# Graph layer on one core: seven of thirteen products of x with Wn1 moved behind all products for A and B

## The reference

```
msg_in   = concat(x[src], x[dst])
h        = relu(relu(msg_in @ Wm1 + bm1) @ Wm2 + bm2)
messages = h @ Wm3 + bm3
agg      = segment_sum(messages, dst) / max(count, 1)
upd      = relu(concat(x, agg) @ Wn1 + bn1) @ Wn2 + bn2
out      = layernorm(x + (x + upd))
```

## Time and profile before

| what | value |
|---|---|
| median of 3 runs | 1199.37 us (1196.93, 1199.37, 1199.49) |
| profiled execution, its time | 1197.71 us |
| its span, first to last instruction | 1195.5 us |
| PE busy | 1159.5 us (97%) |
| DVE busy | 975.5 us (82%) |
| POOL busy | 795.2 us (67%) |
| ACT busy | 743.9 us (62%) |
| mean granted clock of PE | 0.993 |

### The profile page before, as it was taken

The page is one execution under the profiler, slowest core; times in us unless marked ns, Lnnn a source line. Parts: engine busy times, 40 slices in busy tenths (PEclk is TensorE's granted clock), DMA queues, the critical chain, the costliest instruction groups (busy, mean ns, idle before and its releaser), DMA issues.

```text
span 1195.5 us, 33711 instructions
## 1 busy us (share of the span) xinstructions
PE 1159.5 (97%) x9565; PEld 1139.2 (95%) x9566; DVE 975.5 (82%) x2097; ACT 743.9 (62%) x1378; POOL 795.2 (67%) x827
## 2 busy tenths in 40 slices
PE   6888999999999999999999999999999999999996
PEld 6778999999999999999999999999999999999886
DVE  5876877788788888888888888888888888887897
ACT  3555666666666666666666666666666666664674
POOL 2057777777777777777777777777777777773021
PEclk8999999999999999999999999999999999999999
DMA  8876656666565666656666666666555666653022
GB/s 286 306 288 187 179 176 177 176 183 182 180 176 174 180 182 180 181 171 180 182 181 179 174 178 181 178 184 179 175 177 179 181 181 177 174 180 97 19 80 92
DMA packets 136608, 211.47 MB, mean 177 GB/s; under 512 B 25125, under 2 KB 103673, under 8 KB 135034
## 3 DMA queue, kind: packets, MB, share of 16 engines
q1 hardware_dynamic: 99034, 108.50, 29.7%
q0 software_dynamic: 37536, 102.55, 29.0%
HBM read 188.15 MB, written 22.80 MB: 176 GB/s over the span
## 4 chain that ended last, share of the span: by engine, by line
PE 88%; DVE 4%; issue 2%; SPq 2%; POOL 2%; DMA 1%; ACT 0%; DVEq 0%
PE bank L1451 45%; PE bank L1427 14%; PE bank L1338 8%; PE sums L1355 4%; PE sums L1361 4%; PE sums L1359 4%; PE sums L1363 4%; PE bank L1493 2%; POOL a_edge L631 2%; PE bank L1248 1%; DMA a_table<-work 1%; PE sums L1503 1%; PE bank L1233 1%; PE sums L1233 1%; DVE work L1144 1%
## 5 line engine op out<-in xcount | busy, mean ns | idle before, releaser
L631 POOL DMA_INDIRECT a_edge<-a_table,src_idx x782 | 759.7, 971 | 246.7 <-issue 209.9
L1451 PE MATMUL bank<-w,h 128*128 128x256 f32 x4692 | 615.7, 280 | 0.0
L1451 PEld LDWEIGHTS bank<-w,h 128*128 128x128 f32 x4692 | 580.5, 188 | 0.0
L740 ACT ACTIVATE h<-bank 128x512 fp32r<-128x512 f32 x391 | 234.3, 599 | 311.4 <-PE bank L1338 305.2
L1103 DVE SCALAR_TENSOR_TENSOR h<-bank,h 128x512 fp32r<-128x512 f32 x391 | 269.1, 688 | 108.8 <-ACT h L740 72.6
L1115 DVE SCALAR_TENSOR_TENSOR h_lo<-bank,h_hi 128x512 fp32r<-128x512 f32 x391 | 266.6, 682 | 0.0
L729 ACT COPY bank<-b_bc 128x512 f32<-128x512 f32 x391 | 231.6, 592 | 51.4 <-DVE h_lo L1115 46.5
L1427 PE MATMUL bank<-ident,a_edge 128*128 128x128 f32 x1564 | 235.2, 273 | 7.0 <-DVE onehot_t L1020 5.6
L748 ACT ACTIVATE h_hi<-bank 128x512 fp32r<-128x512 f32 x391 | 233.2, 596 | 2.8 <-PE bank L1451 2.8
L1020 DVE TENSOR_SCALAR onehot_t<-rel,node_half 128x256 fp32r<-128x256 int16 x391 | 143.9, 368 | 67.6 <-DMA b_win<-b_table 52.2
L1338 PE MATMUL bank<-onehot_t,b_win 128*128 128x256 f32 x782 | 189.5, 323 | 0.0
(11 more groups left out here) (188 smaller groups left out, 682.4 us busy)
## 6 DMA issues: line engine op xcount, KB each, us to landing
b_win<-b_table SPq DMA_DIRECT2D x391, 128.0 KB
rel<-rel_dram SPq DMA_DIRECT2D x196, 128.0 KB
a_edge<-a_table,src_idx POOLq DMA_INDIRECT x782
a_table<-work SPq DMA_DIRECT2D x12, 512.0 KB, 4.3
b_table<-work SPq DMA_DIRECT2D x5, 1024.0 KB, 5.4
b_table<-h SPq DMA_DIRECT2D x4, 1024.0 KB, 5.5
f_x<-in_x SPq DMA_DIRECT2D x12, 256.0 KB, 5.8
b_table<-a_edge SPq DMA_DIRECT2D x3, 1024.0 KB, 6.1
```

What stands on the lines that cost most here:

```text
L631: pool.indirect_dma_start(a_edge[:, b % R * TB + t, :], None, a_table, bass.IndirectOffsetOnAxis(ap=src_idx[:, b * TB + t:b * TB + t + 1], ...
L740: act.activation(h1[:, k % U, 0, :], bank[k % 2][:, :], ACT.Relu).then_inc(s_h1h, 1)
L1451: ins = pe.matmul(to, h1[:, j, a, h * EB + t * P:h * EB + (t + 1) * P], w2[:, b, h, :], start=False, stop=(a == 1 and h == KH - 1), skip_g ...
```

## The change

Groups 0 to 5 of x @ Wn1 are still made inside the setup's iterations, one each in 5, 7, 8 and 9 and two in iteration 6. Groups 6 to 12 stand behind all products for A and B: groups 6, 7 and 8 ahead of the product W3 x Wn1, groups 9 to 12 behind it. They use banks 6 and 7 and banks 2 and 3 in turn, so that a product waits for the copies of the one before the last. The wait for the last copy of A (s_ac) stands ahead of group 7 now. SP waits for the product of group 6 before it loads windows of B, since the ring of windows holds that group's split x.

```diff
-        TWICE = (XA, XA + 3)
+        EARLY = NG - XB
+        X_AT = {XA: [0], XA + 1: [1, 2], XA + 2: [3], XA + 3: [4], XA + 4: [5]}
         def x_groups(g):
-            done = max(g - XA, 0) + sum(XA <= t < g for t in TWICE)
-            return list(range(done, NG if g == NG else min(done + 1 + (g in TWICE), NG))) if g >= XA else []
-        X_LAST = [NG - 1, NG - 2, NG - 3]
+            return X_AT[g] if g in X_AT else []
+        X_LAST = [k for k in range(EARLY, NG)]
         def x_banks(k):
-            return (2, 3) if k == NG - 2 else (6, 7)
+            return (2, 3) if k >= EARLY and (k - EARLY) % 2 else (6, 7)
...
             sp.wait_ge(s_rw, 11)
+            sp.wait_ge(s_hx, x_nth(XB - 1))
...
-                if k in X_LAST[1:]:
+                if k == EARLY + 1:
+                    pe.wait_ge(s_ac, NPAIR)
+                elif k > EARLY + 1:
                     pe.wait_ge(s_hxa, 2 * (x_nth(k) - 2))
...
-                    x_product(X_LAST[0])
-                    pe.wait_ge(s_ac, NPAIR)
+                    for k in X_LAST[0:3]:
+                        x_product(k)
                     pe.wait_ge(s_w3c, 1)
...
-                    x_product(X_LAST[1])
-                    x_product(X_LAST[2])
+                    for k in X_LAST[3:]:
+                        x_product(k)
```

More of the change, by code:

```diff
@@ L334, in b_groups @@
             return [NG - 2, NG - 1] if g == NG else [g - 1] if 1 <= g < NG - 1 else []
-        TWICE = (XA, XA + 3)
+        EARLY = NG - XB
+        X_AT = {XA: [0], XA + 1: [1, 2], XA + 2: [3], XA + 3: [4], XA + 4: [5]}
+        assert EARLY == 6 and NG > XA + 4 and all(g < XB + k for g, groups in X_AT.items() for k in groups)
         def x_groups(g):
-            done = max(g - XA, 0) + sum(XA <= t < g for t in TWICE)
-            return list(range(done, NG if g == NG else min(done + 1 + (g in TWICE), NG))) if g >= XA else []
-        X_LAST = [NG - 1, NG - 2, NG - 3]
-        assert x_groups(NG) == sorted(X_LAST) and all(g >= XB + x for x in range(NG - 3) for g in (XB + x,)
-                                                      if x not in x_groups(g))
-        X_ORDER = [k for k in range(NG - 3)] + X_LAST
+            return X_AT[g] if g in X_AT else []
+        X_LAST = [k for k in range(EARLY, NG)]
         def x_banks(k):
-            return (2, 3) if k == NG - 2 else (6, 7)
+            return (2, 3) if k >= EARLY and (k - EARLY) % 2 else (6, 7)
         def x_nth(k):
-            return X_ORDER.index(k) + 1
+            return k + 1
         BOTH = (NG - 4) // 3 * 3
```

## The result

The median is 1200.41 us (20 runs, 1198.14 to 1204.99) against 1198.66 for the kernel before (20 runs, 1196.93 to 1200.11): a ratio of 1.0017 with a 95% interval of 1.0009 to 1.0025, by which it is 2.0 us slower (1.1 to 3.0). This is clear of the noise. The forecast of 1.2 us more lies inside the interval, 0.8 us under the measured value. The changed kernel's runs spread over 6.9 us, those of the kernel before over 3.2 here and over 4.3 to 5.9 in the later comparisons, with 35 runs each.

What follows compares the result with a forecast made beforehand. POOL's gathers were taken to set the loop's start; with a longer PE tail, their wait for block 0 outweighs starting 0.5 us earlier: +1.2 us, 1198.9 from the profiled execution, put at 1199.9 by earlier runs, range 1197.0 to 1202.4.

Steps and rivals of the forecast that it cites:

- The gathers 0.5 us earlier: End of setup: A's last copies and store come 0.4 to 0.5 earlier, so POOL's gathers begin at about 81.1.
- PE's tail: Behind B of group 12: four more products, 4 x 1.49 us; last setup matmul starts at 89.8 instead of 85.41.
- DVE's entry: Between clearing and first one-hot matrix: DVE's registers and loads come into the open, taken at 1.15 us.
- The new wait: POOL's ninth gather waits until PE has expanded block 0, going at 93.3 instead of 92.06: +1.2 us.
- Block 10: Main loop: the delayed gather chain starts block 10's transposes at 116.6 instead of 115.41.
- The half clock at the loop's start: PE's half clock from 90.9 to 94 goes away, worth nothing because the gathers set the pace.
- The order of products 1 and 2: Swapped in iterations 5 and 6: product 2's later ACT copies hold up transposes, 0.2 us (bounds 0 and 0.7).
- Rival 1: Ahead of B of group 12: clock falls, half-clock stretch costs 1.55 us, +2.75 in all, 1201.2; chance 0.18.
- Rival 2: At DVE's loop entry: it takes 2.69 instead of 1.15, +1.55 more, 1201.2; chance 0.08.
- rival 3: Setup: A and B really come forward, last store moves with PE; -4.4 us, 1194.0; chance 0.06.
- rival 4: Loop start: PE starts early enough, only the earlier gathers count, -0.5 us, 1197.9; chance 0.10.
- The gap of 2.64 us: PE's gaps in iterations 10 to 13: in the earlier trace the clock fell after a gap this long or longer.

Runs made afterwards that it cites:

- the one with the words moved: Kernel before with five of DVE's instructions on the words (2.3 us) in iteration 7 instead of 8: 1198.23 us, ratio 0.9994.
- the words' run: Changed kernel with five of DVE's instructions on the words (2.3 us) in iteration 7 instead of 8, nothing else: 1200.07 us, ratio 1.0004.
- the matmul ahead: Changed kernel with PE's last setup matmul ahead of the last four products instead of behind them: 1200.37 us, ratio 1.0004 to the kernel before.

## Why the prediction was right

**The gathers 0.5 us earlier: right in this profile.** From the edge transposes, which it put 0.2 later, to the first gather the forecast gave 0.7 less; the changed kernel takes 0.52 less (36.62 against 37.14). Profiles differ by as much: two more kernels with the products as before take 36.71 (the one with idle matmuls and the one with the words moved). DVE's timeline shows the waits that the sum spoke of:

```profile
73.06 1.27 DVE L973 TENSOR_TENSOR work<-bank,rel 128x512 f32<-128x512 f32 x2
...
75.98 1.29 DVE L973 TENSOR_TENSOR work<-bank,rel 128x512 f32<-128x512 f32 x2 [0.26 <-DMA a_table<-work]
...
79.64 0.42 DVE L973 TENSOR_TENSOR work<-bank,rel 128x256 f32<-128x256 f32 x1 [2.37 <-DMA a_table<-work]
```

The wait for PE of the earlier trace rows is gone, and what is late next is the store, now with 2.37 us of idleness on DVE; its landing took 5.19 instead of 4.71. The 6 us taken off PE's way bought half a microsecond at most. The reason given for it, that DVE alone is full, looks too narrow by the profiles: with 2.3 us less on DVE in iteration 8 the gathers came hardly earlier (in the four kernels with the words moved, 36.7 to 37.8 from the edge transposes to the first gather; 36.6 to 37.1 in the kernel before, the changed one and the one with the old order). By the times of the words' run alone (1.0004) this stays open.

**PE's tail: right.** From the first gather to the last setup matmul 8.7 us were forecast (81.1 to 89.8), 8.35 came (84.06 to 92.41). **DVE's entry: mis-sized.** Taken at 1.15, it is 0.61; the clearing began 0.73 instead of 0.45 behind the start of the matmul. **The new wait: right.** POOL's ninth gather was forecast 12.2 behind the first (81.1 to 93.3) and went at 11.75, against 10.43 before. The trace shows this wait (1.66 to 3.10) in all five kernels that keep seven late products with the matmul behind them, and hardly or not at all (0.30 to 0.51) in the five with the products in other places or the matmul ahead, whose loop begins within 9.3 us of the first gather; without groups 9 to 12, where DVE comes late, it is 1.25. What the tail costs shows best in the stretch from the first gather to block 11. It takes 36.34 to 36.60 in the three profiles with the products in their places of before, 37.55 to 39.40 in those five with the tail (37.58 in the changed kernel's), and 36.65 to 37.97 in the three with seven late products and the matmul ahead. So the tail costs 1.0 us in the changed kernel's profile and up to 3 in others. Moving the matmul ahead took off 1.3 and 1.1 per mille in two pairs of kernels, together 1.2 with some 1.0 of uncertainty by the intervals. That the tail costs a microsecond or more is thus likely by the times, and shown as a mechanism by the traces.

**Block 10: right in sign, too large in size.** From the edge transposes to block 10 it takes 71.63 instead of 70.92: +0.7, where +1.0 had been forecast (1.2, less the 0.2 of the order); to block 11 it is +0.46. The forecast took over the way from the ninth gather to block 10 "as now". But in the kernel before, that way went through DVE's entry into its loop (2.69), for which PE waited 0.72 ahead of block 10; in the changed kernel PE comes to block 10 without a wait, and from block 9 to block 10 it takes 2.56 instead of 3.44.

**The half clock at the loop's start: right.** It is gone in the changed kernel's profile, and it was worth nothing: in the kernel before with idle matmuls it lasted 10.4 us, from 89.3 on, and the stretch from the first gather to block 11 takes 36.58 there, against 36.60 with 3.5 us of half clock.

**What was left out of the sum.** The measured 2.0 is 0.8 us more than was forecast, while the forecast's own steps came to only 0.46 in the one profile of the changed kernel. So the mechanism was right, and that the number came as near has a part of luck. Three things can fill the difference. The tail took up to 1.8 us more in other profiles than in this one. The order of products 1 and 2, priced at 0.2, cost 0.3: from product 0 to the edge transposes four profiles with the old order and full clock there take 11.66 to 11.69, four with the new one 11.98 to 12.01 (14.24 and 14.63 at half clock). And falls of the clock were a rival with 0.18, for one gap. Between 40 and 85 us they stand in six of the eight profiles with the new order of products 1 and 2 (at 48 to 50 in four, 67 to 68 in three, 80 in two), and in none of the six with the old order, though not in the changed kernel's own profile. From the edge transposes to the first gather these six take 37.26 to 39.18, and the other eight 36.57 to 37.30. So the order probably brings both. Its price by the times isn't settled: the old order gave 1.0012 and the filled gaps of iteration 7 1.0013, whose intervals overlap that of 1.0017, and how the difference divides stays open. Rival 1, the fall ahead of B of group 12, came in two other kernels' profiles and not in this one, where the gap was 1.87 instead of the 2.4 forecast. Rival 2 fell with the entry of 0.61, rival 3 with gathers that came half a microsecond earlier and not over two, rival 4 because the loop's start counted.

## What to carry to other kernels

Work moved behind a hand-over fills the hole there only up to its size: ask what stands behind the moved work on every engine, here a matmul that released DVE's set-up, and put that release ahead of the filler. Taking work off an engine that isn't the last to finish in a stage moves the stage by its own small wait, and leaves gaps in which its clock can fall. Where runs of one kernel differ by more than the change, compare stretches between marks in the traces and not the marks themselves, and do it over several profiles: the steps of the change came to 0.46 us in one profile, and the times gave 2.0.

## What the runs showed of the hardware

That filling one gap doesn't settle the clock was not expected: in the four kernels with idle matmuls in iterations 3 to 5 it fell at 26 to 28, and with idle matmuls in iteration 7 at 66.7 and 80.4. In the stretches ahead of such falls PE had been busy for 1.51 of 3.3 us, 1.68 of 4.4 and 1.01 of 2.6, in pieces and not at rest. The gap of 2.64 us that the forecast took as its mark was neither needed nor enough. In the rows at 80.4 the longest gap ahead of the fall is one of 1.79 us; in the changed kernel's profile PE waited 2.79 us ahead of its row at 67.43, and the granted clock stayed at 1.00.
